# Attention beside a feed-forward layer: the third tile row of the probabilities turned by VectorE's squares and transfers

## The reference

```python
qu, ku, vu, qc, kc, vc = split(xn @ W_qkv.T)          # qu and qc scaled by 1/8
term1     = where(mask, 0.0, qc @ vu.T)
lookahead = where(mask, sigmoid(qu @ ku.T), 0.0)
Su        = term1 @ lookahead.T
scores    = where(mask, -max, qc @ kc.T - silu(Su))
out       = softmax(scores) @ vc                       # heads joined, then @ W_out.T
ffn       = (silu(xn @ wg.T) * (xn @ wu.T)) @ wd.T     # wg, wu, wd: integers / 127
```

## Time and profile before

| | us |
|---|---|
| median of 3 runs (lowest, highest) | 1092.63 (1091.49, 1093.06) |
| the profiled execution | 1095.02 |
| its span | 1093.1 |
| TensorE busy (matmuls) | 1064.7 |
| VectorE busy | 866.9 |
| ScalarE busy | 756.1 |
| GpSimd busy | 573.1 |

### The profile page before, as it was taken

One profiled execution on the slowest core, in us unless ns is written; L12 is line 12 of the kernel. 1 busy time (PEld: TensorE's weight loads), 2 busy tenths in 40 slices (PEclk: granted clock), 3 DMA queues, 4 the chain that ended last, 5 costly groups with the idle time before them and its releaser, 6 DMA issues.

```text
span 1093.1 us, 21638 instructions
## 1 busy us (share of the span) xinstructions
PE 1064.7 (97%) x7652; PEld 944.6 (86%) x7652; DVE 866.9 (79%) x1832; ACT 756.1 (69%) x1483; POOL 573.1 (52%) x629
## 2 busy tenths in 40 slices
PE   6999999999999999999999999999999998999998
PEld 5888888888888888888888888888888877989997
DVE  5787788878888888788878887888777777476766
ACT  5677777777777777777777777777777775344333
POOL 4356565556555655565556555655555555422240
PEclk9999999999999999999999999999999999999999
DMA  5032434334433443343324433433324546546641
GB/s 192 1 78 63 102 103 105 79 83 122 109 76 77 127 83 99 78 130 79 98 72 130 90 93 74 131 86 80 97 59 130 181 134 212 173 167 208 214 144 59
DMA packets 241932, 120.72 MB, mean 110 GB/s; under 512 B 162464, under 2 KB 221088, under 8 KB 239776
## 3 DMA queue, kind: packets, MB, share of 16 engines
q1 hardware_dynamic: 241824, 119.32, 40.0%
HBM read 64.75 MB, written 54.53 MB: 109 GB/s over the span
## 4 chain that ended last, share of the span: by engine, by line
PE 81%; DVE 7%; POOL 5%; ACT 4%; issue 2%; DMA 0%; DVEq 0%; POOLq 0%; ACTq 0%
PE X L832 21%; PE X L747 16%; PE X L985 8%; PE X L976 7%; PE X L816 6%; PE X L884 5%; PE X L786 5%; POOL prob L667 5%; PE X L800 5%; PE X L866 4%; PE X L771 3%; ACT T_s L1149 1%; DVE L_s L1452 1%; DVE prob L1482 1%; DVE PT_s L1528 1%
## 5 line engine op out<-in xcount | busy, mean ns | idle before, releaser
L667 POOL TENSOR_SCALAR prob<-prob,inv 128x512 f32<-128x512 f32 (+3 forms) x256 | 310.5, 1230 | 33.0 <-DVE inv L1494 33.0
L832 PE MATMUL X<-L_s,T_s 128*128 128x128 f32 (+3 forms) x1920 | 283.5, 302 | 7.8 <-DVE L_s L1452 3.6
L832 PEld LDWEIGHTS X<-L_s,T_s 128*128 128x128 f32 x1920 | 264.6, 189 | 28.4 <-issue 20.1
L747 PE MATMUL X<-xT,W 128*128 128x512 f32 (+1 forms) x972 | 244.7, 399 | 0.0
L747 PEld LDWEIGHTS X<-xT,W 128*128 128x128 f32 x972 | 175.7, 191 | 40.9 <-issue 0.4
L1163 ACT ACTIVATE gate<-X 128x1024 f32<-128x1024 f32 (+1 forms) x96 | 84.8, 884 | 167.2 <-PE X L832 167.2
L1466 DVE SCALAR_TENSOR_TENSOR gate<-gate,X 128x1024 f32<-128x1024 f32 (+1 forms) x96 | 99.7, 1039 | 101.3 <-ACT gate L1163 101.3
L641 POOL TENSOR_SCALAR_AFFINE_SELECT gate<-gate 128x256 f32<-128x256 f32 (+1 forms) x96 | 47.7, 496 | 200.5 <-DVE gate L1466 200.5
L657 POOL TENSOR_SCALAR_AFFINE_SELECT T_s<-T_s 128x512 fp32r<-128x512 f32 x128 | 104.8, 831 | 81.2 <-DVE T_s L1459 81.2
L1171 ACT ACTIVATE prob<-prob,least 128x512 f32<-128x512 f32 (+3 forms) x256 | 141.9, 589 | 1.5 <-DVE least L1482 1.5
L1482 DVE CUSTOM_DVE_ANT_0 prob<-X,gate 128x512 f32<-128x512 f32 (+3 forms) x256 | 112.6, 487 | 14.5 <-PE X L816 12.3
(11 more groups left out here) (108 smaller groups left out, 1883.8 us busy)
## 6 DMA issues: line engine op xcount, KB each, us to landing
heads_out<-o_s SPq DMA_DIRECT2D x62, 256.0 KB, 3.3
prob_raw<-prob SPq DMA_DIRECT2D x240, 64.0 KB, 1.9
PT_s<-prob_raw SPq DMA_DIRECT2D x120, 128.0 KB, 2.4
xT_copy<-xT SPq DMA_DIRECT2D x8, 1024.0 KB, 6.8
w_split<-w_parts SPq DMA_DIRECT2D x22, 256.0 KB, 2.5
W<-w_split SPq DMA_DIRECT2D x12, 384.0 KB, 6.3
xT<-xT_copy SPq DMA_DIRECT2D x4, 1024.0 KB, 5.6
tanh_l<-in_L_attn_x SPq DMA_DIRECT2D x8, 512.0 KB, 4.8
```

Of the source, the lines that this page charges most:

```text
L667: last = pool.tensor_scalar(v, v, inv[:, h, w - 1:w], None, ALU.mult)
L747: last = pe.matmul(out[:, tokens], sh.W[:, a, k, cols], xT[:, c, k, tokens], start=(n == 0), stop=(n == 3 * KD - 1))
L832: last = pe.matmul(both[:, h, at:at + (J + 1) * P], T_s[:, h, a, to:to + P], L_s[:, h, c, WIDE[J + 1]:WIDE[J + 1] + (J + 1) * P], start=(J ...
```

## The change

In words:

- Row 2 (queries 256 to 383), three blocks a head, now goes the way of row 3: squares on VectorE, 8 transfers out, 3 back (`spread_row` with I = 3 and I = 2). SP does row 3, the stores of o, then row 2. `high_rows` on ScalarE waits for both rows and copies them in two pieces, 1536 and 256 elements a partition; `low_rows` on VectorE subtracts.
- TensorE turns the three blocks of rows 0 and 1 of both heads at once, after the first sums (`turn_heads`): 6 transposes a step instead of 12. `high_heads` and `low_heads` handle them once a step.
- `TURNS`: the first sums move from banks 6 and 7 to banks 2 and 3, the second from 2 and 3 to 6 and 7; the second turn is gone.
- VectorE's order: the subtractions of QU and KU and the squares of row 3 move behind the last part of L_s; row 2's squares stand behind QC; `take_low_max` stands before the first silu. `minus_scores` of group 1 waits until row 2's transfers have landed.
- x is spread in 4 transfers and loaded in 2. One piece of W (`POOL_PIECES`) moves from VectorE to GpSimd before the steps.
- Around the last pair: other banks, the first half of the heads loaded earlier, and in `ffn_second` the first two `project_o` between the `gate_up`.

The diff, cut to its core:

```diff
-POOL_PIECES = (0, 1, 3, 4, 5)
+POOL_PIECES = (0, 1, 3, 4, 5, 6)
@@ TURNS
-         ("Su", 0, (6, 7)), ("PH", 0, (0, 1)), ("PT", 0, (0, 1)), ("PT", 1, (4,)), ("Su", 1, (2, 3)),
-         ("PH", 1, (6, 7)), ("PT", 2, (6, 7)), ("Su", 2, (4, 5))]
+         ("Su", 0, (2, 3)), ("PH", 0, (0, 1)), ("PT", 0, (0, 1)), ("PT", 1, (4,)), ("Su", 1, (6, 7)),
+          ("PT", 2, (2, 3)), ("Su", 2, (4, 5))]
@@ SP: step
                 if back1 and g - 1 < SQUARED:
-                    spread_last_row(g - 1, back2)
+                    spread_row(g - 1, 3, back2)
                 if back2:
                     store_o(g - 2, q % 2)
+                if back1 and g - 1 < SQUARED:
+                    spread_row(g - 1, 2, back2)
+
+            def spread_row(g, I, attended):
+
+                sp.wait_ge(row_in_squares_done[I], g + 1)
+                sp.sem_inc(ticks, 1)
+                raw, at, n = prob_raw[I][g], WIDE[I + 1], 4 * (I + 1)
                 for h in range(2):
                     for i in range(4):
+                        sp.dma_start(raw[h].rearrange("q r t -> r q t")[:, :, i * 32:(i + 1) * 32],
+                                     prob[i * 32:(i + 1) * 32, h, at:at + n * 32].rearrange("r (q t) -> r q t", t=32)) \
+                          .then_inc(row_spread[I], 16)
+                sp.wait_ge(row_spread[I], (g + 1) * 8 * 16)
                 if attended:
                     sp.wait_ge(o_filled, 2 * g)
+                for K in range(I + 1):
+                    sp.dma_start(PT_blocks[:, :, LOW, WIDE[TT - K] // P + I - K, :],
+                                 raw[:, 4 * K:4 * K + 4, :, :].rearrange("h q r t -> (q r) h t")) \
+                      .then_inc(row_loaded[I], 16)
@@ SP: before the feed-forward part
+            load_o(0, (1,))
             load_xT(1)
             sp.wait_ge(scores_emptied, after(LAST_G, 2))
-            load_o(0)
+            load_o(0, (0,))
@@ TensorE
+            def turn_heads(part, b, g):
+
+                pe.wait_ge(prob_ready, after(g - 1, 2))
+                tile = take_bank(part, b, g, "PH", 0)
+                for h in range(2):
+                    for i, (K, I) in enumerate([(0, 0), (0, 1), (1, 1)]):
+                        last = pe.transpose(tile[:, h, i * P:(i + 1) * P],
+                                            prob[:, h, WIDE[I + 1] + K * P:WIDE[I + 1] + (K + 1) * P], ident[:, :])
                 last.then_inc(PT_filled, 1)
@@ ScalarE
+            def high_rows(g):
+
+                for I in (3, 2):
+                    act.wait_ge(row_loaded[I], (g + 1) * (I + 1) * 16)
+                act.activation(three_pairs(HIGH).bitcast(F32R), three_pairs(LOW), ACT.Copy).then_inc(rows_high, 1)
+                act.activation(PT_blocks[:, :, HIGH, 7, :].bitcast(F32R), PT_blocks[:, :, LOW, 7, :], ACT.Copy) \
+                   .then_inc(rows_high, 1)
@@ VectorE: minus_scores
-                        wait_before(dve, last_row_spread, g * 8 * 16)
+                        wait_before(dve, row_spread[3], g * 8 * 16)
+                if j == 1 and 0 <= g - 1 < SQUARED:
+                    wait_before(dve, row_spread[2], g * 8 * 16)
@@ VectorE: step
-                if back1 and g - 1 < SQUARED:
-                    row_in_squares(g - 1)
                 if back1:
                     inverse(g - 1, 1)
-                if ahead:
-                    low_proj(g + 1, QU, par)
                 low_L(g, 1)
-                if ahead:
-                    low_proj(g + 1, KU, par)
...
                 if ahead:
+                    low_proj(g + 1, QU, par)
+                    low_proj(g + 1, KU, par)
+                if back1 and g - 1 < SQUARED:
+                    row_in_squares(g - 1, 3)
+                if ahead:
                     low_proj(g + 1, VU, par)
...
                 if ahead:
                     low_proj(g + 1, QC, par)
+                if back1 and g - 1 < SQUARED:
+                    row_in_squares(g - 1, 2)
```

More of the change, by code:

```diff
@@ L311, in layer @@
         prob_ready = sem("prob_ready")
[L312 to L316, removed]
+        row_in_squares_done = {I: sem(f"row{I}_in_squares") for I in (3, 2)}
+        row_spread = {I: sem(f"row{I}_spread") for I in (3, 2)}
+        row_loaded = {I: sem(f"row{I}_loaded") for I in (3, 2)}
+        rows_high = sem("rows_high")
+        rows_low = sem("rows_low")
         PT_high = sem("PT_high")
@@ L927, in step @@
                 if back1 and g - 1 < SQUARED:
-                    turn_head(part, b, g, 0)
+                    turn_heads(part, b, g)
                 elif back1:
@@ L932, in step @@
                 sum_up(part, b, g, 1)
-                if back1 and g - 1 < SQUARED:
-                    turn_head(part, b, g, 1)
-                elif back1:
+                if back1 and g - 1 >= SQUARED:
                     turn_probs(part, b, g, 2)
@@ L1035, in ffn_second @@
                 g = LAST_G + 1
[L1036 to L1039, removed]
+                gate_up(1, 0, products)
+                gate_up(1, 1, products)
+                project_o(0, 0)
+                project_o(0, 1)
+                gate_up(1, 2, products)
+                project_o(0, 2)
+                project_o(0, 3)
+                gate_up(1, 3, products)
                 down(0, 5, products)
@@ new lines, in row_in_squares, with low_rows @@
+            def row_in_squares(g, I):
+                at = WIDE[I + 1]
+                dve.wait_ge(prob_ready, after(g, 3 - I))
+                dve.transpose(prob[:, :, at:at + (I + 1) * P], prob[:, :, at:at + (I + 1) * P]).then_inc(row_in_squares_done[I], 1)
+            def low_rows(g):
+                dve.wait_ge(rows_high, 2 * g + 1)
+                dve.tensor_tensor(three_pairs(LOW).bitcast(F32R), three_pairs(LOW), three_pairs(HIGH), ALU.subtract) \
+                   .then_inc(rows_low, 1)
+                dve.wait_ge(rows_high, 2 * g + 2)
+                dve.tensor_tensor(PT_blocks[:, :, LOW, 7, :].bitcast(F32R), PT_blocks[:, :, LOW, 7, :],
+                                  PT_blocks[:, :, HIGH, 7, :], ALU.subtract).then_inc(rows_low, 1)
@@ L1785, in build @@
     xT_copy = [nc.dram_tensor(f"xT_copy{b}", [P, 2, KD, SEQ], F32).ap() for b in range(BATCH)]
-    xT_raw = [nc.dram_tensor(f"xT_raw{b}", [KD, P, SEQ], F32).ap() for b in range(BATCH)]
-    prob_raw = [nc.dram_tensor(f"prob_raw{g}", [2, 16, 32, P], F32).ap() for g in range(SQUARED)]
+    xT_raw = [nc.dram_tensor(f"xT_raw{b}", [TT, 8, 32, P], F32).ap() for b in range(BATCH)]
+    prob_raw = {I: [nc.dram_tensor(f"prob_raw{I}_{g}", [2, 4 * I + 4, 32, P], F32).ap() for g in range(SQUARED)] for I in (3, 2)}
     heads_out = nc.dram_tensor("heads_out", [2, BATCH * INNER, SEQ], F32).ap()
```

146 lines of the change are left out of this document (58 added, 88 removed).

## The result

The changed kernel takes **1220.20 us** (median of 4 runs, 1219.05 to 1225.26); the kernel before took 1092.66 in the same session. The ratio is 1.1178, 95% interval 1.1145 to 1.1211. The direction was forecast and the size was not: 1152 was predicted, the range ended at 1180, and of the predicted loss of 59 us there came 127.5.

A forecast was written before the change was run, and what follows sets the result against it. TensorE, busy 97%, bounds the kernel before; after the change SP's loop was to set 29.15 + 0.4, about 29.6 us a step. 29 steps give plus 58, small parts plus 1: 1152 us on the median's footing, range 1120 to 1180.

The forecast's parts named there:

- SP's loop through both rows: Attention steps: ScalarE's copy, VectorE's squares, SP's transfers and loads of rows 3 and 2 close a loop setting the step.
- most signs that were named for it: Changed profile: copy waits 2 to 3 us every step, TensorE waits before the attention product, steps 29 to 30 us.
- The first rival: Attention steps: the loop does not bind, steps fall to TensorE's 26.6 or about 27.0 us; 1072 us, chance 12%.
- the sum of the loop, 29.15 + 0.4: Attention step: ScalarE and VectorE 11.3 us, SP 17.85, sum 29.15; 0.4 added for slow moments gives 29.6 a step.
- 5.5 for eight transfers of row 2 and their landing: SP's part of the loop, behind the stores of o: issuing row 2's eight transfers and their landing take 5.5 us.
- the 0.4 for hiccups: SP in the loop: 0.4 us a step added because stores or loads sometimes took 1.0 to 1.3 us above usual.
- 1 us of SP's bad moments in each step: Upper bound of the loop: with this and 0.4 on the copy, 30.5 us a step, 1178, rounded to 1180.
- The rival of collisions: SP's transfers: short packets slow each other, three landings cost 1 us more in half the steps; 31.1, 1195 us, 7%.
- The small parts: Outside the loop: x's transfers, the last attention step, the work behind it and the moved piece of W; together plus 1.
- 3 of at most 4: Behind the last attention step: new order and an earlier load win back 3 us of at most 4 lost by TensorE.
- The clock: TensorE's waits each step bring 1.2 GHz, costing 1.7 us that the loop hides; twice a step gives 1167 us, 6%.
- VectorE's wait for row 2's transfers: VectorE before overwriting row 2's squares: transfers land at about 7.1 of the step, it writes at 7.2; cost nothing.

The follow-up runs named there:

- e6: The changed kernel with stores of o behind row 2, row 3's squares right behind the reciprocals, and rows copied and subtracted earlier: 1082.81 us, ratio 0.9905.
- e7: e6 with the 1 MB load of x for the first feed-forward block issued one step earlier, ahead of row 2's transfers: 1078.94 us, ratio 0.9869.
- e2: The changed kernel with SP storing o behind row 2's transfers instead of ahead of them: 1158.55 us, ratio 1.0602 to the kernel before.
- e1: The changed kernel with VectorE squaring row 3 directly behind the first part of L_s, as before the change: 1110.51 us, ratio 1.0160.
- e3: The changed kernel with the edits of e1 and e2 together: 1103.48 us, ratio 1.0101 to the kernel before.
- e5: e3 with row 3's squares behind the second group of reciprocals instead of ahead of it: 1086.89 us, ratio 0.9945 to the kernel before.

## Why the prediction was wrong

**What held.** The mechanism: SP's loop through both rows sets the step, and most signs that were named for it are there (the copy waits in every step, by 4.2 us instead of 2 to 3; TensorE's wait moved to the attention product; the transposes are gone). One is not: SP was to issue or wait for landings "through nearly the whole step", but it waits for row 3's squares by 361.4 us in 30 times, one of them 47.6, which leaves 10.8 a step. The sum itself had given 11.3 of the loop to ScalarE and VectorE. TensorE's own way was 26.6, or 27.0 as a mean of four, and e6 and e7, where the copy waits for its loads in at most three steps, give 26.86 in a plain step and 27.1 as a mean: close to the mean, 0.26 above in the plain step. The first rival's 1072 us for a loop that does not bind was a fair size; e7 takes 1079. It belonged to a kernel whose loop is loose, and this one's was not.

**What failed: the sum of the loop, 29.15 + 0.4.** Means of 28 turns in the changed kernel, beside the terms of the prediction (which sum to 29.15 there, by rounding):

```text
term                                   predicted  measured
ScalarE's copy to its third L_s copy      8.15      8.12
VectorE to the end of the squares         3.17      3.46
to the first issue                        0.10      0.09
8 issues of row 3 and their landing       5.55      6.12
4 loads and the stores of o               3.34      3.46
8 issues of row 2 and their landing       5.50      6.89
3 loads to the copy's start               3.36      3.70
sum                                      29.17     31.84
extra for SP's bad moments                0.40        -
```

The step that failed is "5.5 for eight transfers of row 2 and their landing". It was priced like row 3's, with a shorter wait because the pieces are fewer. Its issues took 5.42 on average, not about 4.1. This one term is 1.39 of the 2.67 that the sum was short, 40 us of the time. Part of its excess is its place right behind the stores of o, 0.86 on its first two issues; e2 moves the stores away and it goes. The rest of the excess was to be covered by the 0.4 for hiccups and was not: row 3's issues and landing exceeded their term by 0.57, the landing of the last load by 0.34, and VectorE's part by 0.29, where the last part of L_s took 0.95 beside GpSimd.

The hiccups come together with something that the prediction did not look at. The page's part 3 lists a second DMA queue, q8, that moves instructions; in the changed kernel:

```profile
q8 instruction: 61, 1.00, 0.4%
```

These are packets of 16 KB (1.00 MB in 61), one about every 20 us. The slow issue at 643.80 (1.25 us for the usual 0.5) has one beside it; so have both slow groups of the earlier trace rows, and the eight issues of the earlier trace rows have none. Part 3 for 643.7:645.1:

```profile
q8 instruction: 1, 0.02, 3.9%
```

In 28 steps of the changed kernel row 3's eight issues took 4.15 us without such a packet beside them and 5.19 with one (7 of the 28), row 2's 4.92 and 5.76 (16 of 28); the wait from the last issue until all have landed was 1.46 and 3.23 for row 3 (4 of 28), 1.36 and 2.90 for row 2 (2 of 28). Spread over the 28 steps that is 1.1 us each, beside the 0.86 of the stores. Over all nine kernels, 92 issues of squares behind the second of their eight took over 0.9 us, and 86 of them have a packet of q8 beside them, against 64 of the 2794 shorter ones. That the packets are the cause is likely but argued: no run moved them. From SP's first issue to the next copy every turn of the changed kernel has one or two of these packets, so a hiccup like those of the earlier trace rows falls on nearly every turn, and the prediction spread them thin, as 0.4.

The bound above, "1 us of SP's bad moments in each step", was short as well: it gave 30.5. The rival of collisions gave 31.1 by three landings of plus 1 us in half of the steps. The mean is above that too, and its excess is mainly issue time and not landings.

**The small parts**: plus 1 was forecast, and 5.6 came (plus 7.2 behind the steps, minus 1.6 ahead of them). The last step was to start its sums "3 to 4 us later". They start at 28.58 of that step instead of 16.80, because its gate and up products wait for the load of x:

```profile
1004.36 3.78 PE L981 MATMUL X<-xT,W 128*128 128x512 f32 x8 [10.09 <-DMA xT<-xT_copy]
```

That load stands in SP's program behind row 2 and was overlooked: the prediction went through what row 2 delays in the loop and not through everything else behind it on the queue. e7 shows it by moving that load alone: the rest is 8.3 us shorter in the profiled execution, though the medians are only 3.9 apart. Of the 11.8 us by which the sums are late, 7.2 are left at the end. The 4.6 between are put down to the new order of the feed-forward part, where 3 of at most 4 were forecast: no wait like the 2.24 at 924.63 of the earlier trace rows is left, but no run took the new order out.

**The clock** as forecast cost nothing visible. In the steps the mean granted clock is 0.95 (1.00 in the earlier trace rows). TensorE's weight loads waited 3.82 us before the attention product at 655.99, and the window behind that wait shows 0.53, nearly all of it at the lower level of 1.2 GHz:

```profile
655.99:662.80 6.81, 6.78 (x27) 6.42 (x28) 5.68 (x13) 6.21 (x18) 4.80 (x4) 0.53 0.19 82
```

The path from the copy to ScalarE's third L_s, which would feel a late TensorE, stayed between 8.11 and 8.13 us in all 28 turns. So the page on the clock (the Trainium skill, TensorE: Matmul & The Clock Gate, HAM oscillation) is right that recurring waits bring the low clock back, and the loop hid its price. That is read from the trace; no run kept the clock up while the loop stayed.

**VectorE's wait for row 2's transfers** was costed at nothing. It is a real wait, 42.1 us in 27 times, and TensorE waits behind it by 33.3 us in all before the VU and QC projections, whose banks the second scores hold. Almost none of it is on the chain, so in time it was nothing.

**Issue time.** Row 2's eight issues take 5.70 us at 640.89 and one lands in 2.1 us by the page's part 6. The sentence of the Trainium skill that issuing "is usually small relative to the DMA itself" (DMA: Bandwidth & Descriptors, Issuing engines are not separate DMA queues) is written for one transfer, and here one issue of about 0.5 us is a quarter of its landing. But eight issues on one queue add up while their landings overlap, so the sentence is no guide to a series: SP's issues have 30% of the chain, landings 17%.

**What bounds next**, which e1's and e3's expectations missed. With the loop loose the step stood at 27.9, not at 26.6, held by GpSimd's probabilities. ScalarE's longer copy, which the prediction had noted as standing ahead of the exponentials, and squares ahead of the reciprocals each push GpSimd, the engine nearest to the path in the earlier trace rows. e5 shows the second by 0.68 us a step. The first is argued only, since no run split the copy. The 27.6 of every fourth step in e5 to e7 is put down to VectorE's turn of x, and was not tested.

## What to carry to other kernels

When work is moved to a queue, write the loop through the queue from one use to the next, and price each group of issues at its new place with what stands directly ahead of it, not at the price it has alone. If the trace before shows slow moments on that queue, find what runs beside them and count how often it will fall into a loop that has no slack. The order on the queue was worth 2.3 us a step and the place of one 1.23 us pass on another engine 3.75. Then list everything that stands behind the new entries on that queue in every stage, the last one above all. A loop that costs as much as the whole change may be loosened by order alone: four moves that add nothing turned plus 11.8% into minus 1.3%.

## What was not expected of the hardware

- Two stores of 256 KB each make the small issues right behind them slower: the first two of eight take 1.81 us instead of 0.95 (the changed kernel and e2). With 1 MB ahead eight took 6.85, in one step only (e7): one of them 2.31 with no instruction packet beside it, another 1.12 with one.
- Issues that take 1 to 2 us instead of 0.5 come nearly always together with a 16 KB packet of the instruction queue q8 (86 of 92).
- VectorE's L_s passes stretch GpSimd's, while its transposes into squares, as long as they are, do not: a pass of 384 elements takes up to 2.55 us beside L_s in e3 and 1.24 otherwise (1873 ns is the mean of both), and 1.24 to 1.25 beside the squares in the changed kernel. In the other direction, the third part of L_s took 0.95 us at 628.43 for 0.67 in the earlier trace rows. The Trainium skill (SBUF — State Buffer, Who interferes with whom) says that a VectorE instruction with two SBUF inputs contends with a GpSimd instruction that reads SBUF, and that one with a single SBUF input, outside certain modes, does not; L_s has two and the squares one, so the traces agree.
